# A piece of the value projection moved ahead of the second tile's scores in TensorE's order

## What is computed

```python
def local_attention(q, k, v):            # windows of 32, each looks at itself and the one before
    sim = jnp.einsum('bhwie,bhwje->bhwij', bq, bk2) * QK_SCALE
    sim = jnp.where(mask, -jnp.finfo(sim.dtype).max, sim)
    attn = jax.nn.softmax(sim, -1)
    out = jnp.einsum('bhwij,bhwje->bhwie', attn, bv2)
...
qkv = x @ Wqkv                           # q, k: normalised per head, scaled, rotated
out = local_attention(q, k, v)
x = out @ Wo + x
x = (a * gelu(gate)) @ W2 + b2 + x       # a, gate = layernorm(shifted x) @ W1 + b1
```

## Time and profile before

| | |
|---|---|
| median of 3 runs | 3323.44 us (3321.95 to 3325.85) |
| the profiled execution | 3348.17 us, of which the span is 3346.3 us |
| PE busy | 3189.6 us (95%) |
| PEld busy | 2280.0 us (68%) |
| DVE busy | 2888.9 us (86%) |
| ACT busy | 2792.8 us (83%) |
| POOL busy | 2681.3 us (80%) |
| granted PE clock, mean | 0.991 |

### The profile page before, as it was taken

How to read it: one execution, slowest core, us unless ns; L and a number is a source line. 1 busy time by engine, 2 the same in 40 slices (tenths; PEclk the granted TensorE clock), 3 DMA queues, 4 the chain that set the end, 5 groups by cost and what they waited for, 6 DMA issues and landing times.

```text
span 3346.3 us, 128353 instructions
## 1 busy us (share of the span) xinstructions
PE 3189.6 (95%) x51488; PEld 2280.0 (68%) x51488; DVE 2888.9 (86%) x5656; ACT 2792.8 (83%) x5313; POOL 2681.3 (80%) x1798
## 2 busy tenths in 40 slices
PE   8999799999999999999999999999999999999996
PEld 5777466776666666666666767777776776666665
DVE  6999788988888888888888889999999998888884
ACT  5776588888888888887888899988999998888884
POOL 1000498999989889988988999999999998898992
PEclk9999999999999999999999999999999999999998
DMA  2000011111211111211111211112211112111112
GB/s 68 0 0 0 1 39 35 35 37 47 59 38 36 40 40 49 51 40 33 34 40 49 51 40 40 40 36 56 49 40 40 40 40 55 44 40 29 38 40 53
DMA packets 127300, 128.92 MB, mean 39 GB/s; under 512 B 62380, under 2 KB 75824, under 8 KB 126832
## 3 DMA queue, kind: packets, MB, share of 16 engines
q1 hardware_dynamic: 123232, 112.38, 13.8%
q10 hardware_dynamic: 3600, 9.50, 0.9%
HBM read 19.04 MB, written 2.10 MB: 6 GB/s over the span
## 4 chain that ended last, share of the span: by engine, by line
PE 88%; issue 4%; DVE 3%; POOL 2%; ACT 1%; DMA 1%; SPq 1%; ACTq 0%; POOLq 0%; DVEq 0%
PE ps L1319 27%; PE ps L1341 11%; PE ps L1334 9%; PE ps L1350 9%; PE ps L1363 8%; PE ps L1311 8%; PE ps L1373 4%; PE ps L1175 3%; PE ps L1167 2%; PE ps L1164 2%; PE ps L1187 1%; PE ps L1160 1%; PE ps L1200 1%; POOL area L452 1%; PE ps L1295 1%
## 5 line engine op out<-in xcount | busy, mean ns | idle before, releaser
L1319 PE MATMUL ps<-Wqkv,xsT 128*128 128x512 f32 x2304 | 1108.0, 603 | 9.0 <-DMA Wqkv<-ffn_Wqkv 3.3
L452 POOL TENSOR_TENSOR area<-area,tab 128x512 f32<-128x512 f32 x768 | 958.3, 1276 | 38.3 <-ACT area L640 37.7
L1319 PEld LDWEIGHTS ps<-Wqkv,xsT 128*128 128x128 f32 x2304 | 392.7, 191 | 312.4 <-issue 201.2
L474 POOL TENSOR_TENSOR area<-area,lsum 128x1024 f32<-128x1024 f32 x192 | 365.4, 1903 | 281.5 <-DVE lsum L938 280.0
L640 ACT ACTIVATE area<-ps 128x512 f32<-128x512 f32 x768 | 455.1, 593 | 33.7 <-PE ps L1319 33.0
L459 POOL TENSOR_TENSOR area<-area 128x1024 f32<-128x1024 f32 x192 | 451.4, 2373 | 5.9 <-DVE area L997 5.5
L459 POOL TENSOR_TENSOR AQb<-AQb,area 128x1024 f32<-128x1024 f32 x192 | 449.8, 2365 | 0.1
L645 ACT ACTIVATE area<-area 128x1024 f32<-128x1024 f32 x384 | 396.5, 1065 | 0.1
L1341 PE MATMUL ps<-Wo,area 128*128 128x128 f32 x3072 | 377.0, 281 | 10.5 <-issue 10.4
L1363 PE MATMUL ps<-kT,area 64*32 64x64 f32 x24576 | 315.1, 225 | 59.8 <-issue 59.2
L1341 PEld LDWEIGHTS ps<-Wo,area 128*128 128x128 f32 x3072 | 357.4, 195 | 20.6 <-issue 11.9
(11 more groups left out here) (124 smaller groups left out, 6559.6 us busy)
## 6 DMA issues: line engine op xcount, KB each, us to landing
BD<-area SPq DMA_DIRECT2D x1440, 64.0 KB, 2.0
Wqkv<-ffn_Wqkv ACTq DMA_DIRECT2D x12, 512.0 KB, 4.4
x2s<-x2s SPq DMA_DIRECT2D x96, 56.0 KB, 2.1
Wo<-ffn_Wo SPq DMA_DIRECT2D x6, 512.0 KB, 5.1
Wqkv<-ffn_Wqkv ACTq DMA_DIRECT2D x12, 256.0 KB, 3.1
W<-ffn_W SPq DMA_DIRECT2D x6, 341.0 KB
x2s<-x2s SPq DMA_DIRECT2D x96, 7.5 KB, 2.1
x2s<-x2s SPq DMA_DIRECT2D x96, 0.2 KB, 1.7
```

What stands on the lines that cost most here:

```text
L452: pool.tensor_tensor(b4[:, :, here], q4[:, :, there], s4[:, :, here], ALU.mult).then_inc((s_bq, s_bk)[j], 1)
L474: pool.tensor_tensor(p3, p3, lsum[:, 1, :].unsqueeze(2).broadcast_to([P, HEADS, 2 * WIN]), ALU.mult).then_inc(s_pn, 1)
L1319: mm(home(kind + part), xsT[:, par, t * P:(t + 1) * P], Wqkv[:, w0:w0 + 512], start=True, stop=True).then_inc(done, 1)
```

## The change

In TensorE's step, `project(n-1, "V", "01")` moves from behind the four `output` calls to just ahead of `scores(n-1, 1)`. Since it now writes bank 0 before the `output` calls have waited for that bank's eviction, it gets a wait of its own for the second `o_evac` of unit n-2. No instruction of another engine moves, and nothing is added or removed besides that wait.

```diff
@@ -1476,6 +1476,8 @@
                     need_apart(pe, i_pe, s_half, 2 * (n - 2) + 2)
                     values(n - 2, 1, 1, par)
                 if one:
+                    need(pe, s_oe, 4 * (n - 2) + 2)
+                    project(n - 1, "V", "01", old)
                     scores(n - 1, 1)
                 if two:
                     if static and u == 2:
@@ -1487,8 +1489,6 @@
                     need(pe, s_oe, 4 * (n - 2) + 4)
                     output(n - 2, 0, 1)
                     output(n - 2, 1, 1)
-                if one:
-                    project(n - 1, "V", "01", old)
                 if now:
                     need(pe, s_n0, 2 * n + 1)
                     turn(n, "k01")
```

## The result

| | median of the runs, us | range | profiled execution, us | its span |
|---|---|---|---|---|
| before, same session | 3324.64 (4 runs) | 3321.95 to 3342.85 | 3348.17 | 3346.3 |
| after | 3459.74 (4 runs) | 3450.43 to 3467.4 | 3467.4 | 3465.6 |

The kernel is slower by a factor of 1.0393, with an interval of 1.0347 to 1.0439. The direction was forecast, the size was not: 3390 us was the forecast, 3425 the end of the range, and the time lies 35 us above that end. Between the two profiled executions the change cost 119 us, of which the forecast had 67.

The account below looks back on a forecast made before the run. TensorE, busy 95% of the span, was taken as the bound, with loops through VectorE and SP closing. Steps of 30.58 us, less covered second-tile stops, summed by stretches to +67 us: 3323.4 + 67 = 3390 us, range 3350 to 3425.

Parts of the forecast that it names:

- The new wait: TensorE ahead of moved V01: waits for the second output eviction, cold start included, 0.50 us a step, bounds 0.39 and 0.70.
- at either place: V01 in TensorE's step: costs 0.86 us at its old and new place alike, so moving it saves nothing.
- The two loops: Output start (A) through VectorE to `turn_xn`, and through SP's band transfers to `values`: both close, step 30.58 us.
- The band chain: Output start (A) through VectorE's turn and SP's 15 band transfers: holds `values` until A + 20.47 on average, and decides.
- the layer norm: VectorE's chain from output start (A), done at A + 11.97: holds `turn_xn` until A + 12.02.
- k00's turn behind V01's eviction: Ahead of `turn_xn`: the turn of k00 waits for ScalarE's eviction of V01, perhaps 0.2 us, absorbed in `turn_xn`'s wait.
- Rival 1: Only TensorE's own work counts, other engines' chains have slack: sum +12 us, 3335 us; chance 0.10.
- The second tile's stops: Stops in the second tile's scores over 33 steps: V01 and its wait cover them, 35.0 us shrinking to 5.
- Rival 3: The second tile's stops don't give way, so the 33 steps pay 1.24 us too: +108 us, 3431 us; chance 0.11.
- GpSimd's wait for `soft_sum`: GpSimd's `normalise`: waits about 1.2 us longer for `soft_sum`, and has the room for it.
- The first tile's stops: Stops in the first tile's scores: they stay; the wait of `turn_xn` may cover 0.3 to 0.5 us of them.
- From the profile to the median: Whole run: the profiled execution stays 24.7 us above the median, so 3348.2 to 3415 profiled means 3390 us.

Follow-up runs that it names:

- al2_early: `early` with 80 idle increments ahead of the first step and 3 ahead of `values` in each step, pinning block borders; 3344.3 us, ratio 1.0029.
- al2_after: The changed kernel with 80 idle increments ahead of the first step and 3 ahead of `values` in each step; 3386.06 us, ratio 1.0148.
- al2_mid: `mid` with 80 idle increments ahead of the first step and 3 ahead of `values` in each step; 3346.31 us, ratio 1.0041.
- mid: The kernel before with V01 and its wait put between the second tile's scores and the output products; 3458.06 us, ratio 1.0371.
- al_after: The changed kernel with 65 idle increments ahead of the first step and 3 at the start of each step; 3634.67 us, ratio 1.0883.
- early: The changed kernel with ScalarE's second output eviction of unit n-2 put ahead of K10's eviction; 3412.66 us, ratio 1.0234.
- bad_after: The changed kernel with 251 idle increments ahead of the first step and 3 at the start of each step; 3742.68 us, ratio 1.1203.
- wait_only: The kernel before with only the new eviction wait ahead of the second tile's scores, V01 left in place; 3388.47 us, ratio 1.0159.
- al_before: The kernel before with 65 idle increments ahead of the first step and 3 at the start of each step; 3419.27 us, ratio 1.0243.
- bad_before: The kernel before with 251 idle increments ahead of the first step and 3 at the start of each step; 3490.13 us, ratio 1.0447.
- part 3: Kernels before, after, `wait_only`, `mid` and `early`, each with 80 idle increments first and 3 ahead of `values` per step; medians 3274.29 to 3386.06 us.
- al2_before: The kernel before with 80 idle increments ahead of the first step and 3 ahead of `values` in each step; 3274.29 us, ratio 0.9823.

## Why the prediction was wrong

The accounts can now be drawn up against a step without any stop, 29.44 us before and 30.59 after. What each stretch has above that is what stops and clock cost it:

| | before, us | after, us | difference | forecast |
|---|---|---|---|---|
| the change's own price, 93 steps | | | 93 x 1.15 = +107 | 93 x 1.24 = +115 |
| steps 0 to 7 | 4 | 7 | +3 | -1 |
| steps 8 to 40 | 44 | 6 | -38 | -41 |
| steps 41 to 49 | 10 | 7 | -2 | 0 |
| steps 50 to 68 | -1 | 6 | +7 | 0 |
| steps 69 to 76 | -2 | 22 | +23 | 0 |
| steps 77 to 92 | 29 | 47 | +19 | -7 |

- **The new wait: right within its bounds, the middle value low.** The idle time is 0.36 us in every step, where 0.39 was the lower bound, but the scores start 1.49 us later behind `values` and not 1.36. Wait and start together are 0.43 us, and V01 takes 1.06 us at its new place: that V01 costs the same 0.86 us "at either place" is wrong by 0.20. With the 0.20 the sum is 0.63, inside the 0.39 to 0.70. `al2_early` has the 0.20 without any wait, so it isn't what a wait does to the weights, as the prediction put it.
- **The two loops: right that they close, and the sum right partly by luck.** The step was worked out as 20.47 + 8.75 + 1.36 = 30.58 us; without stops it takes 30.59. The parts are less exact than their sum, and their errors of 0.12 and 0.13 us cancel: `values` start at A + 20.35 and not 20.47, and from `values` to A it is 10.24 and not 10.11. The clean step before was 29.44 and not 29.34, so the price is 1.15 and not 1.24. The band chain decides over `values`, as forecast. `turn_xn` was put at A + 12.02 and stands at A + 12.11, but the layer norm is not what mostly holds it: `turn_xn` starts 0.06 us behind its end in 16 of 93 steps of `al2_after` and about 0.15 in the others. The 0.3 us that TensorE loses on the way are ahead of q01's turn, for `residual1`. The prediction had 0.2 us for k00's turn behind V01's eviction; in `al2_mid` that eviction is over at least 1.0 us ahead of k00's turn, and the 0.3 us are there all the same. Rival 1, only TensorE's own work, falls: it would have been 0.5 us a step.
- **The second tile's stops: right.** They were to shrink from 35 us to 5, and what stretch 8 to 40 has above a clean step went from 44 us to 6. Rival 3 falls. `mid` shows the cause: with V01 behind these scores most of them stay. (A slip without weight: the stops of the first steps are in the first tile's scores in one step only, 1.4 us, and in the L1311 products behind them in three, where the prediction has "five"; and the 1.87 us that it reads from the earlier trace rows is 1.82 there.)
- **GpSimd's wait for `soft_sum`:** forecast longer by 1.2 us a unit, measured (381.9 - 280.0) / 96 = 1.06. It cost nothing, as forecast.
- **The first tile's stops: wrong, and this is the step that failed.** The prediction said that they "stay", that "their block contains `turn_xn`, whose wait may cover 0.3 to 0.5 us of them", and that the 27 steps from 1977.61 on stay without stops, since before they had none. Measured: +19 us instead of -7 in the last 16 steps, +23 in the 8 ahead of them, +7 in the 19 ahead of those. The mistake is one of symmetry. I moved V01's 0.86 us into the block ahead of one border and asked what that covers; I did not ask what it uncovers at the border that it left. TensorE now reaches the first tile's scores 0.35 to 0.58 us sooner after A, the packet does not come earlier for it (A + 13.1 and later in both kernels where there is a stop), and the stop is longer by as much. In the steps 69 to 75, moreover, the packet itself came at A + 13.1 to 13.4, where before it came at A + 5.7 to 6.7, and there a stop of 1.9 to 2.8 us is all new. So what symmetry explains are the longer stops where there were stops before; the new ones, 23 of the 52 us by which the forecast fell short, come from the packet's move, and why it moved is not known (below).
- **The clock: missing from the prediction.** It fell in 6 of the 93 steps of before, which I had not seen, and I had no term for it. After, it falls in 20. Fourteen steps more at 1.7 us are 24 us, about half of the 49 that stops and clock add in the last three rows of the table.
- **From the profile to the median:** I took the 24.7 us by which the profiled execution of before stood above its median as constant. That of after stands 7.7 above its own. So the median rose by 135 us where the profiles differ by 119, and 17 of the 70 us by which 3390 fell short come from this.

**What stays open.** Two things. First, what sets the time of the packet. The ones that feed the first tile's scores came at A + 5.4 to 6.7, at A + 7.7 to 8.9, at A + 10.2 to 12.2 or behind A + 12.9 (in some kernels and steps also between A + 1.6 and 4.2); in none of the fourteen traces came a packet between A + 8.9 and A + 10.2. The first band transfer is issued at A + 8.0 to 8.3 in most steps. The stops go with the packets behind A + 12.9, with one exception (`al_after`, a packet at A + 11.4 and 0.8 us of idle time). That fits a request that either goes ahead of the band transfers or gets stuck with them, but the runs show only that three instructions in another place of the step, with the border nearly the same, turn late packets into early ones in all 93 steps (88 up to A + 6.7, five at A + 8.6 to 8.9). No run took the band transfers away. Second, why the clock falls behind nearly every stop of after and behind one in five of before, at the same length of stop. The kernels in which it falls most (`after`, `mid`, `early`, `bad_after`: 19 of 21, 16 of 26, 14 of 19, 93 of 93) are, with `al_after` (58 of 64), those with the short wait ahead of the turn of q01; with V01 behind the outputs it is 3 of 14 in `before`, 5 of 15 in `wait_only`, 13 of 63 in `al_before`, 20 of 93 in `bad_before`. That is a coincidence over the kernels, not a cause shown: the wait is there in nearly every step of `after`, `mid` and `early`, also in those in which a stop leaves the clock as it was.

## What to carry to other kernels

Work that is moved in a list lengthens the stretch ahead of one point and shortens that ahead of another: account for both, at every point where the engine can be held up from outside, the ends of instruction blocks among them. Where a step that is written out for all units is a few instructions short of a whole number of blocks, its stops wander through the program and a fix in one place comes back as a cost in another; pinning the border (here 3 idle instructions a step, in the right place) took 58 us off the kernel before, 1.8% (3274.29 against 3331.88 us in the same set), and made the experiments of part 3 readable, since each then had nearly one step length. In another place of the step the same three instructions cost 2.4%. Before a small edit is judged on such a kernel, measure it with the borders pinned: the change here costs 1.15 us a step by itself and between 0 and 4 us a step by where the borders happen to be.

## What the runs showed of the hardware

- TensorE stood for 0.3 to 3.0 us (idle time) at a border of 256 instructions in a run of small matmuls. The 128 records of one call of scores, as many as a block holds, are used up in 1.48 us. Whether it stood went with the packet of the instruction queue: at A + 5.5 no stop in step 60 of before, at A + 13.0 a stop of 1.8 us in step 60 of `al_before`, with the border behind the same record.
- A stop of about 2 us can bring the granted clock down to 0.50 for 3.41 us. It did so behind 17 of 63 stops in one kernel and behind 39 of 39 of like length in the other. Where it falls, a stop costs nearly twice its length.
- The wait of TensorE for the same eviction was 0.36 us ahead of a projection and 0.61 us ahead of the scores. The same projection took 0.86 us behind the output products, 0.96 behind the scores (`al2_mid`) and 1.06 behind `values`, waiting or not.
- 251 increments in a row on TensorE's queue took 38.4 us, 0.15 us each. In `al2_before` the 80 ahead of the first step are some 12 us of its 3274, which a cheaper filling at that place could save; this wasn't tried.
